# List rounds at every second attention step, experts eight in three steps, three more tiles rotated by GpSimd

## The reference

```python
x = L0_attn_x                                   # 4 x 512 x 256
xn = _layernorm(x)
x = x + _L0_attn_ref(xn, ...) + _L0_ffn_ref(xn, ...)
xn = _layernorm(x)
x = x + _L1_attn_ref(xn, ...) + _L1_ffn_ref(xn, ...)

# _L0_attn_ref: 16 heads of 16, 4 key/value heads, rotary positions,
#   window of 64 keys and 16 meta keys, softmax, output product Wo
# _L0_ffn_ref: 64 experts, 8 for each token, at most 128 tokens for an expert
logits = x @ router_weight.T
topw, topi = jax.lax.top_k(softmax(logits), 8)
pos = rank of the token in its expert's list    # cumsum of the one-hot choices
xe[expert, pos] = x                             # pos >= 128 is dropped
ye = (silu(xe @ gate) * (xe @ up)) @ down       # 256 -> 96 -> 256
y = sum over the 8 experts of ye * weight
```

## Time and profile before

| | us |
|---|---|
| median of 3 runs | 1325.66 (1323.35 to 1326.56) |
| the profiled execution | 1328.68 |
| its span | 1326.9 |
| mean granted PE clock in it | 0.972 |

### The profile page before, as it was taken

The page is one execution under the profiler, slowest core; times in us unless marked ns, Lnnn a source line. Parts: engine busy times, 40 slices in busy tenths (PEclk is TensorE's granted clock), DMA queues, the critical chain, the costliest instruction groups (busy, mean ns, idle before and its releaser), DMA issues. The chain is left out here.

```text
span 1326.9 us, 21489 instructions
## 1 busy us (share of the span) xinstructions
PE 1249.4 (94%) x7794; PEld 1077.9 (81%) x7829; DVE 691.9 (52%) x1390; ACT 535.3 (40%) x1173; POOL 672.0 (51%) x532
## 2 busy tenths in 40 slices
PE   6588999999979998999999999999999997999997
PEld 5467888888858887888788888888888885899996
DVE  7994555555676577675654435434343334522234
ACT  4475566666555333334233343333343333311111
POOL 3635778876203565676666556566555551010023
PEclk9698999999998998999999999999999998999998
DMA  9603778886705211121222112111211105389943
GB/s 320 202 1 86 177 169 183 184 174 131 175 1 171 68 45 47 61 64 48 80 64 70 53 38 68 53 52 37 65 43 45 37 13 173 118 294 335 332 151 113
DMA packets 111208, 150.65 MB, mean 114 GB/s; under 512 B 12192, under 2 KB 92192, under 8 KB 110976
## 3 DMA queue, kind: packets, MB, share of 16 engines
q1 hardware_dynamic: 94064, 121.09, 27.9%
q0 software_dynamic: 17040, 28.19, 10.7%
HBM read 121.29 MB, written 27.95 MB: 112 GB/s over the span
## 5 line engine op out<-in xcount | busy, mean ns | idle before, releaser
L1596 PE MATMUL a_p_p<-a_xr,a_wr 128*128 128x512 f32 x1152 | 308.7, 403 | 2.4 <-DVE g_x L2146 2.4
L1596 PEld LDWEIGHTS a_p_p<-a_xr,a_wr 128*128 128x128 f32 x1152 | 206.6, 189 | 42.6 <-DVE g_x L2146 3.1
L1914 POOL TENSOR_TENSOR a_sqsum<-a_sqsum,a_sq 128x512 f32<-128x512 f32 x60 | 77.9, 1298 | 232.5 <-ACT a_sq L1799 232.5
L1882 POOL TENSOR_TENSOR a_wr<-g_hold,a_wr 128x768 fp32r<-128x768 f32 x63 | 122.4, 1942 | 19.7 <-DVE a_wr L1946 19.7
L1982 DVE SCALAR_TENSOR_TENSOR a_gated<-a_th,a_p_o 128x512 f32<-128x512 f32 x64 | 44.0, 688 | 159.3 <-ACT a_sq L1799 159.3
L404 POOL DMA_INDIRECT acc<-l_ye,g_slot_token x64 | 104.0, 1626 | 39.4 <-ACT l_ye L753 20.1
L1916 POOL TENSOR_TENSOR a_gr<-a_gated,a_gr 128x512 fp32r<-128x512 f32 x64 | 97.8, 1528 | 23.7 <-DVE a_gr L1986 23.7
L1609 PE MATMUL a_p_p<-a_wvr,a_xr 128*128 128x512 f32 x384 | 108.3, 420 | 0.6 <-DVE a_xr L1940 0.6
L1667 PE MATMUL a_p_w<-a_gr,l_wo_r 128*128 128x512 f32 x384 | 100.7, 397 | 2.3 <-POOL a_gr L1916 2.3
L1180 POOL DMA_DIRECT2D out<-e_ye x23 | 12.5, 545 | 165.4 <-DVE e_ye L1348 165.4
L1651 PE MATMUL a_p_o<-a_sc,a_v 128*128 128x128 f32 x512 | 90.0, 278 | 6.6 <-DVE a_sc L1962 6.6
(11 more groups left out here) (280 smaller groups left out, 2784.3 us busy)
## 6 DMA issues: line engine op xcount, KB each, us to landing
g_hold<-in_Wqkg SPq DMA_DIRECT2D x64, 384.0 KB, 3.2
e_up<-in_gate_up SPq DMA_DIRECT2D x23, 1024.0 KB, 7.0
g_hold<-in_gate_up SPq DMA_DIRECT2D x64, 192.0 KB
e_down<-in_down SPq DMA_DIRECT2D x23, 512.0 KB, 5.2
g_hold<-in_Wv SPq DMA_DIRECT2D x16, 512.0 KB, 4.5
l_down<-in_down SPq DMA_DIRECT2D x64, 96.0 KB
acc<-l_zero SPq DMA_DIRECT2D x2, 2176.0 KB, 11.8
rows<-l_zero SPq DMA_DIRECT2D x1, 2944.0 KB, 21.1
```

The costliest lines, as they stand in the source:

```text
L1596: mm = pe.matmul(dst[:, :], wr[n % 2][:, wp, kk, c * P:(c + 1) * P], xr[n // H1 % 2][:, xp, kk, :], start=(kk, xp, wp) == (0, 0, 0), stop= ...
L1882: pool.tensor_tensor(wr[n % 2][:, 1, :, :], w[n % 2], wr[n % 2][:, 0, :, :], ALU.subtract).then_inc(w_parts, 1)
L1914: pool.tensor_tensor(sqsum[b % 2][:, :], sqsum[b % 2][:, :], sq[a % 2][:, :], ALU.add).then_inc(summed, 1)
```

## The change

It touches only the schedule of layer 0.

- `PICKS`: the 16 rounds stand in the steps -5, -3, -1, 1, 3, ... 25, instead of -5, -4, ... 10.
- `LISTS` is 27 instead of 12, and with it `SCALED`: ACT makes the diagonals of the steps 12 to 26 instead of DVE.
- `TICK0` is 30 instead of 15, and place k stands in step 30 + (3 k) // 8 instead of 15 + k // 2: three, three and two places in three steps. The 66 places take the steps 30 to 54 instead of 15 to 47. In a step with three, PE and ACT do the middle one behind the transposed scores; DVE does the first two together.
- `EARLY` is 9 instead of 6: POOL does the three rotation products and the low parts of tiles 6, 7 and 8, which DVE did.

```diff
--- before.py
+++ after.py
@@ -143,8 +143,9 @@
     SLOTS = G0 + 1
     FIRST, LAST = -9, STEPS + 10
     LEAD = 2
-    EARLY = 6
-    PICK0, LISTS, TICK0 = -5, 12, 15
+    EARLY = 9
+    PICKS = (-5, -3) + tuple(range(-1, 27, 2))
+    LISTS, TICK0 = 27, 30
     TAKEN, IS_TAKEN = -3.0e38, -1.0e38
     TICKS = E0 + 2
     SCALED = LISTS
@@ -275,8 +276,8 @@
             t, r = divmod(n + lead, G0)
             return t if r == 0 and 0 <= t < NT else None
 
-        pick_at = {PICK0 + i: i for i in range(NT)}
-        ticks_at = {n: [k for k in range(TICKS) if TICK0 + k // 2 == n] for n in range(FIRST, LAST)}
+        pick_at = {n: i for i, n in enumerate(PICKS)}
+        ticks_at = {n: [k for k in range(TICKS) if TICK0 + 3 * k // 8 == n] for n in range(FIRST, LAST)}
 
         @block.sync
         def _(sp):
@@ -644,6 +645,8 @@
                     turn_scores(v)
                     if v % G0 == G0 - 1:
                         turn_meta(v // G0)
+                for k in ticks_at[n][1:-1]:
+                    tick(k)
                 if tile_at(v, -4) is not None:
                     values(tile_at(v, -4))
                 if tile_at(v, -5) is not None:
@@ -652,7 +655,7 @@
                     turn_y(tile_at(v, -6))
                 if tile_at(v, -7) is not None:
                     project_y(tile_at(v, -7))
-                for k in ticks_at[n][1:]:
+                for k in ticks_at[n][-1:]:
                     tick(k)
 
         @block.scalar
@@ -1043,13 +1048,13 @@
                     weigh()
                 if 0 <= n < STEPS:
                     maxima(n)
-                for k in ticks_at[n][0:1]:
+                for k in ticks_at[n][:-1]:
                     tick(k)
                 if tile_at(v, -5) is not None:
                     divide(tile_at(v, -5))
                 if tile_at(v, -7) is not None:
                     add_out(tile_at(v, -7))
-                for k in ticks_at[n][1:]:
+                for k in ticks_at[n][-1:]:
                     tick(k)
                 if n in pick_at:
                     pick(pick_at[n])
```

## The result

| | median us | range | ratio to before, 95% interval |
|---|---|---|---|
| before | 1326.11 | 1323.35 to 1326.62 | |
| after | 1356.43 | 1356.31 to 1357.42 | 1.0227 [1.0212, 1.0242] |

What follows compares the result with a forecast made beforehand. Bounds: DVE up to M(15), PE and POOL nearly level through the expert places, then PE. Gains of 10 us in front, less a POOL-paced last scatter and late sums, put layer 0 14.8 us later: 1343.5, less 3.0, 1340.5; range 1329 to 1353.

Steps and rivals of the forecast that it cites:

- The end of layer 0: Steps 59 to 61: sums come 18 us after the last scatter, DVE stands still 8 us; layer 0 ends at 411.8.
- M(15): Start of DVE's maximum (TENSOR_REDUCE of line 959) in step 15, M(n) likewise in step n; 113.84 us before, forecast 103.8.
- Steps 15 to 29 run without experts: M(15) to M(30): 15 steps at PE's 3.62 us are 54.3, taken as 53.0; diagonals and rotation counted as nothing.
- Picks at every second step: Steps up to 11: fewer picks on DVE gain 4.9, 3 and 2 us, in sum 10 us earlier (bounds 5 and 15).
- nothing more up to M(15), where PE is already the limit: Steps 11 to 15: the 10 us gained by step 11 neither grow nor shrink up to M(15).
- POOL's pace: Expert places: a scatter, a gather and 0.30 us ahead of each make 3.24 us an expert; 56 experts take 181.6 us.
- the last seven: Last seven scatters, which have no gathers: about 3.0 us each, 21 us in all (bounds 1.88 and 3.29 each).
- The clock behind the wait: PE at the end of layer 0, behind the 8 us wait: 1 us added for a lower clock.
- 4 us more: By the skill's clock rule, cold work behind the wait and PE's gaps in the experts cost this extra, giving 1344 to 1345.
- (1): Rival, end of layer 0: the stretch grows but sums arrive in time; +5.6 us, 1331; chance 0.11.
- (3): Rival, expert places: POOL isn't the limit, an expert takes under 2.94 us; faster, 1320; chance 0.08.
- (2): Rival, expert places: PE's chains are slower than POOL, 3.4 us an expert; end +27, 1352; chance 0.12.

Runs made afterwards that it cites:

- after, again: The changed kernel, unchanged, run and profiled again later on one of the experiments' chips: 1353.07 us, 1.0253 of the kernel before on that chip.
- the first experiment: The changed kernel with the 16 rounds of picking back at every step, -5 to 10, all else as changed: 1349.46 us, ratio to before 1.0229.
- the pick ahead: The changed kernel with each round of picking moved ahead of the division and the last addition in its step on DVE: 1346.46 us, ratio to before 1.0202.
- removing them together: The changed kernel with picks ahead of the division, only the first eight gathers, and first three sums at steps 62 to 64: 1331.83 us, 1.0089 of before.

## Why the prediction was right in sign and short in size

The end of layer 0 came at 426.6 instead of 411.8, 14.8 us beyond the forecast, and layer 1 was not touched (928 us behind it in after, 930 in before). By stretches: to M(15) 2.5, M(15) to M(30) 9.1, to the first scatter 2.1, first to last scatter 0.2, to the first sum 1.7, behind it -0.9. Nearly all of it lies ahead of the first scatter. The 2.1 us are no error of the forecast: they are the delay at step 30 that only the first profile shows, and in after, again, that stretch took 6.5 us for the 7 forecast. There layer 0 ends at 421.09, 9.3 us beyond the forecast: 4.0, 8.4, -0.5, -3.1, 1.6 and -1.2 by the same stretches.

**The step that failed** is "Steps 15 to 29 run without experts" with "so I take 53.0". Six of the sixteen rounds stand in these steps, and they went into the sum at nothing, without a reason. The part on picks counted what the front gains by their leaving and never what they cost where they go; only ACT's diagonals and the rotation were weighed there, and both are at nothing, as forecast (59.6 us with the diagonals on DVE, 61.7 with the rotation there, among 59.5 to 62.1 without). Without picks these steps take 53.1 us, with them 59.5 to 62.1. What passed for cover, DVE's free time, was there (40.75 of 61.42 us busy), but not where half of the rounds stand. Those in the division's steps (15, 19 and 23) delay the maxima and the division that PE waits for, and behind one to three of the waits in these steps the clock fell as well, which made PE's work 2 to 5 us longer. Three rounds in the other steps of a tile cost nothing in the tile from M(11) (13.73 us against 13.72).

**Picks at every second step**: forecast 10 us by M(11). M(0) was 5.2 earlier (forecast 4.9), the gain at M(11) was 8.1 and at M(15) 7.5. The step "nothing more up to M(15), where PE is already the limit" has the same hole twice: the rounds of steps 11 and 13 are new there, and the turn of the lists leaves steps 12 and 13. M(11) to M(15) is 15.2 us before, 13.7 with neither rounds nor lists in it (the first experiment) and 15.9 in after, so the two rounds cost 2.2 us where what left gave back 1.5. That this is the lists isn't shown apart; the first experiment differs from before in the rotation and the diagonals too.

**POOL's pace**: right. 3.24 us forecast, 3.262 and 3.263 measured. That first to last scatter is 202.8 against 202.6 is partly luck: it is 185.2 to the 57th (181.6 forecast) and 17.6 for the last seven (21), two errors that cancel. In after, again, these are 182.6 and 16.9, and M(30) to M(55) took 205.7 us, the forecast's 362.4 - 156.8 = 205.6. Taking the gathers away brought PE's 3.00. An engine at 51% of the span was the limit of a stretch, and the earlier trace rows were enough to see it.

**The end of layer 0**: right in mechanism, 6.43 us of waiting for 8. From the last scatter to the first sum it was 19.7 us for 18, since the first addition landed 11.4 us after its issue (388.77 to 400.13) and not 10. The clock behind the wait was charged at 1 us. By the rule of the Trainium skill, "TensorE: Matmul & The Clock Gate", section "HAM oscillation — how this bites in real kernels", that the work behind a wait starts cold, the prediction estimated 4 us more. The trace agrees with its direction: behind the wait of 6.98 us two products of line 510 take 0.87 us, 0.52 ahead of it. But from the first sum to the end it was 26.5 us, 26.4 before, since before had its own stretch at the lower clock there (0.89 in the earlier trace rows, 0.88 in after). The 4 us more were not seen at this place.

The clock counted elsewhere. From M(15) to M(30) it was 0.92 in both profiles of after, and PE was busy for 4.2 us longer than with the pick ahead, which neither of the prediction's two sums had at this place. In the two other traces of the same code it was 0.97, and PE's work 1.5 us longer.

**The rivals.** (1), sums in time, fell: the wait is there. (3), faster with scatters under 2.94 us, fell: 3.26. (2), chains of PE at 3.4 an expert, fell as a mechanism, since POOL sets the pace, although the time it named, 1352, was nearer to the result; the size came from another place. No one of the three costs found makes up the loss: removing them together gives back 21 of 33 us, and of the 12 left some 6 are PE busy for longer, unexplained.

**What the forecast didn't say**: that the rate alone loses. Before with three places in a step is 1.5% slower. The forecast had the two prices, 25.9 us of POOL against 22.7 of PE for eight experts, and used them only for the date of the last scatter. It never said that PE would stand idle by it (14.6 us from M(15) to M(40) in that kernel) and have attention left over afterwards. The cost is in the forecast's time all the same.

## What to carry to other kernels

Time an engine is idle is not time that more work on it can use: look at which instruction stands behind the new one in its queue, who waits for that, and whether PE's clock falls behind the wait. The same work can be dear in one step and free in the next. When work is moved from a crowded stretch to an easy one, price it where it arrives as well as where it leaves. Where two engines run at nearly the same pace, crowding the work of one makes the other wait for it and leaves its own work for later, alone.

## What the runs showed of the hardware

- An indirect scatter took POOL 1555 ns on average with no gathers between and 1624 (after) and 1650 (before) with them, a gather 1026 and 992 ns; 0.30 us stood ahead of each with nothing late.
- PE's clock fell behind waits of 1.47 and 1.5 us in some executions and not behind the same waits in others: from M(15) to M(30) it stood at 0.92 in both profiles of after, and at 0.97 in the kernels with eight gathers and with later sums, with nearly the same waits. After 3.42 us of waiting (175.61 in after) two products of line 585 took 1.22 us and eight of line 593 1.91, where the same took 0.61 and 1.04, as at 1.2 instead of 2.4 GHz.
- The step at which the places begin took 14.4 us in the first profile of after (M(30) to M(31)) and 8.2 in every later one with places from step 30. Before shows as much in its first three steps of places (22.4 against 16.0 us). The cause wasn't found; the kernels are the same.
EOF
